# Slot experts: a ring of eight weight buffers that SyncE alone loads, and expert outputs stored by ScalarE

## The chip, the cores and the metric

The kernel runs on one core of one Trainium2 chip. The metric is the device time of one execution, in microseconds (us). PE is TensorE, ACT is ScalarE, DVE is VectorE, POOL is GpSimd and SP is SyncE. Each core has 16 DMA engines. SP, ACT and POOL can each issue a DMA: an instruction that hands the transfer over and returns, with a semaphore raised when the data has landed.

## The reference, cut to what matters

The model is a two-layer audio tower: seven convolutions with layer norms, a state space layer, a routed mixture of 4 experts, a two-way scan, and last a soft mixture of 64 experts. Only the last part is touched. Each expert `n` works on 16 slots of each of 8 batches, so on 128 rows of 192 features:

```python
Xs = jnp.einsum('bmd,bmnp->bnpd', x, D)
hdn = _layernorm(Xs, ln_g[:, None, :], ln_b[:, None, :])
hdn = jnp.einsum('bnpd,ndh->bnph', hdn, w1) + b1[:, None, :]     # 192 -> 384
hdn = jax.nn.gelu(hdn, approximate=False)
Ys = jnp.einsum('bnph,nhd->bnpd', hdn, w2) + b2[:, None, :]      # 384 -> 192
Y = jnp.einsum('bsd,bms->bmd', Ys.reshape(bsz, n * p, d), C)
```

## The kernel before

The program is a sequence of blocks, each with one hand-written instruction stream per engine and a barrier at its end. `dispatch` makes the normalised slot inputs (the tiles `H1`, `H2`), `experts` runs the 64 experts, `combine` mixes their outputs into the result. The change is in `experts`, and makes two of its tiles larger.

An expert's weights come in two transfers, issued by SP in `load` (L1808, L1810): `w12` (480 KB: 128 rows of 3840 bytes, the first 128 rows of w1 and all of w2) and `w1x` (97.5 KB: 65 rows of 1536 bytes, the rest of w1 and the bias row). They go to slot `r` of a ring of `RING = 4`; each slot has a semaphore `expert_loaded{r}`.

Per expert, DVE scales the slot inputs into `a1`, `a2` (L1907). PE does `up(n)`: six matmuls into one of two PSUM banks (L1850, L1851), raising `expert_hid`. ACT does the GELU into `eg` (L1877), raising `expert_act`. PE does `down(n)`: three matmuls (L1858), raising `expert_out`; ACT copies the result from PSUM to slot `r` of `ye` (L1883), raising `expert_read`. The tile goes to `ys` in HBM (L1822, 96 KB). In each stream the order is fixed: PE does `up(n+1)` and then `down(n)`; ACT does the GELU of n+1 and then the copy of n. The copy first waits until the store of expert n-4, from the same slot of `ye`, has landed (`y_stored{r}`). `down(n)` waits for the GELU of n and for the copy of n-2.

SP's loop body for one expert is: wait for `expert_out` of n, load expert n+4 into the slot that is now free, wait for the copy of n, store n. As PE goes to `up(n+4)` after `up(n+3)` and `down(n+2)`, weights are issued some two experts' time before they are wanted.

POOL meanwhile fetches parts of `ectb` (375 KB each, 12 in all) that `combine` will need (L1840). `combine` starts with three loads of `yb` from `ys`, issued by ACT (L1925), and so needs all stores to have landed.

Of the kernel before, what the change touches and what calls it, by code (L numbers as in the profile page):

```python
# [12 lines left out]
P = 128  # L13
B = 8
# [540 lines left out]
D = 192  # L555
D1, D2 = 128, D - 128
# [10 lines left out]
SOFT_E, SLOT, SOFT_H = 64, 16, 384  # L567
SLOTS = SOFT_E * SLOT
SC = SLOTS // P
SHC = SOFT_H // P  # L570
# [1222 lines left out]


RING = 4
MIX_PIECES = 4
MIX_RING = 3


def experts(nc, T, S, io):  # L1800

    ps = T["ps"]
    pH, pY = [ps[0], ps[1]], [ps[2], ps[3]]
    W = SOFT_H + SHC * D
    n_rows = B * SLOT

    def load(sp, n, r):
        sp.dma_start(T["w12"][:, r, :], bass.AP(io["w12"].tensor, n * P * W, [[W, P], [1, W]]))\  # L1808
            .then_inc(S[f"expert_loaded{r}"], 16)
        sp.dma_start(T["w1x"][:, r, :], bass.AP(io["w1x"].tensor, n * (D2 + 1) * SOFT_H, [[SOFT_H, D2 + 1], [1, SOFT_H]]))\  # L1810
            .then_inc(S[f"expert_loaded{r}"], 16)

    with nc.Block() as block:
        @block.sync
        def _(sp):
            for r in range(RING):
                load(sp, r, r)
            def store(sp, n, r):
                sp.wait_ge(S["expert_read"], n + 3)

                dst = bass.AP(io["ys"].tensor, n * SLOT * D, [[SLOTS * D, B], [D, SLOT], [1, D]])
                sp.dma_start(dst, T["ye"][:, r, :]).then_inc(S[f"y_stored{r}"], 16)  # L1822
            with sp.Fori(0, SOFT_E - 2 * RING + 1, RING) as i:
                for r in range(RING):
                    sp.wait_ge(S["expert_out"], i + r + 1)
                    load(sp, i + r + RING, r)
                    store(sp, i + r, r)
            for r in range(RING):
                store(sp, SOFT_E - RING + r, r)
            for r in range(RING):  # L1830
                sp.wait_ge(S[f"y_stored{r}"], 16 * SOFT_E // RING + 16)

        @block.gpsimd
        def _(pool):

            for n in range(MIX_RING * MIX_PIECES):
                pool.wait_ge(S["expert_out"], SOFT_E * (n + 1) // (MIX_RING * MIX_PIECES + 1))
                b, c = n // MIX_PIECES, n % MIX_PIECES * (SC // MIX_PIECES)
                s = slice(c, c + SC // MIX_PIECES)
                pool.dma_start(T["ectb"][:, b, s, :], io["ect"][b][:, s, :]).then_inc(S[f"mix_ahead{b}"], 16)  # L1840

        @block.tensor
        def _(pe):
            def up(n, r, loaded):
                pe.wait_ge(S[f"expert_loaded{r}"], loaded)
                pe.wait_ge(S["slots_ready"], 2 * n + 2)

                for c in range(SHC):
                    o = pH[r % 2][:, c * n_rows:(c + 1) * n_rows]
                    pe.matmul(o, T["w12"][:, r, c * P:(c + 1) * P], T["a1"][:, r, :], start=True, stop=False)  # L1850
                    mm = pe.matmul(o, T["w1x"][:, r, c * P:(c + 1) * P], T["a2"][:, r, :], start=False, stop=True)  # L1851
                mm.then_inc(S["expert_hid"], 1)

            def down(n, r):
                pe.wait_ge(S["expert_act"], n + 1)
                pe.wait_ge(S["expert_read"], n + 1)
                for c in range(SHC):
                    mm = pe.matmul(pY[r % 2][:, 0:D], T["eg"][:, r % 2, c * n_rows:(c + 1) * n_rows],  # L1858
                                   T["w12"][:, r, SOFT_H + c * D:SOFT_H + (c + 1) * D], start=(c == 0), stop=(c == SHC - 1))
                mm.then_inc(S["expert_out"], 1)  # L1860

            def products(i, last=False):
                for r in range(RING):
                    if not (last and r == RING - 1):
                        ahead = (r + 1) // RING
                        up(i + r + 1, (r + 1) % RING, 32 // RING * i + 32 * (1 + ahead))
                    down(i + r, r)
            up(0, 0, 32)
            with pe.Fori(0, SOFT_E - 2 * RING + 1, RING) as i:
                products(i)  # L1870
            products(SOFT_E - RING, last=True)

        @block.scalar
        def _(act):
            def gelu(n, r):
                act.wait_ge(S["expert_hid"], n + RING + 1)
                act.activation(T["eg"][:, r % 2, :], pH[r % 2][:, 0:SHC * n_rows], ACT.Gelu)\  # L1877
                    .then_inc(S["expert_act"], 1)

            def copy(n, r, stored):  # L1880
                act.wait_ge(S["expert_out"], n + 1)
                act.wait_ge(S[f"y_stored{r}"], stored)
                act.activation(T["ye"][:, r, :], pY[r % 2][:, 0:D], ACT.Copy).then_inc(S["expert_read"], 1)  # L1883

            def activations(i, last=False):
                for r in range(RING):
                    if not (last and r == RING - 1):
                        gelu(i + r + 1, (r + 1) % RING)
                    copy(i + r, r, 16 // RING * i + 16)
            gelu(0, 0)  # L1890
            with act.Fori(0, SOFT_E - 2 * RING + 1, RING) as i:
                activations(i)
            activations(SOFT_E - RING, last=True)

        @block.vector
        def _(dve):

            dve.sem_inc(S["expert_hid"], RING)
            dve.sem_inc(S["expert_read"], 2)
            for r in range(RING):  # L1900
                dve.sem_inc(S[f"y_stored{r}"], 16)
            with dve.Fori(0, SOFT_E - RING + 1, RING) as i:
                for r in range(RING):
                    dve.wait_ge(S["expert_hid"], i + r + 1)

                    for name, src, g, rows in (("a1", "H1", "egA", P), ("a2", "H2", "egB", D2)):
                        dve.tensor_scalar(T[name][0:rows, r, :], T[src][:, bass.ds((i + r) * n_rows, n_rows)],  # L1907
                                          T[g][:, 0, bass.ds(i + r, 1)], T[g][:, 1, bass.ds(i + r, 1)], ALU.mult, ALU.add)\
                            .then_inc(S["slots_ready"], 1)


def combine(nc, T, S, io):

    pO = T["ps"][0:2]
    with nc.Block() as block:
# [24 lines left out]
        def _(dve):  # L1940
            def bias(b):
                if b < MIX_RING:
                    dve.wait_ge(S[f"mix_ahead{b}"], 16 * MIX_PIECES)
                dve.wait_ge(S[f"mix_loaded{b % MIX_RING}"], 16 + 32 * (b // MIX_RING))  # L1944
# [30 lines left out]
def program(nc, io):  # L1975
    with ExitStack() as ctx:
# [4 lines left out]
        T, S, made = {}, {}, []  # L1981
# [4 lines left out]
        for name in ("nvar nroot tok_link tok_turned tok_normed tok_back tok_affine tok_projected tok_out "  # L1986
                     "ssm_exp ssm_r ssm_angle ssm_link u_ready u_turned uT_ready ssm_in Bu_ready x_ready "
                     "ssm_out y_ready ssm_nlink ssm_slink ssm_blink rows_loaded weights_loaded small_loaded readout_loaded v_ready "
                     "v_turned vT_ready scores_ready mask_ready "
                     "z_ready ez_ready gate_link xh_ready xh_turned two_out "  # L1990
                     "n_ready proj_read proj_done conv_read conv2_done y2_ready two_done two_nlink two_link "
                     "sig phi_link phi_sum phi_root q_ready lg_read q_turned qT_ready "
                     "lg_done xs_read edt_ready lt_done ht_read ed_read ed_turned ect_read ect_turned xs_done "
                     "hat_ready xs2_padded ht_done lg_max lt_max ect_stored0 ect_stored1 xvar xroot soft_nlink rzd_ready "
                     "xs_link expert_out slots_ready expert_hid expert_act expert_read y_stored0 y_stored1 y_stored2 y_stored3 "
                     "soft_loaded mixed mix_out stored0 stored1 stored2 stored3 yb_ready mix_loaded0 mix_loaded1 mix_loaded2 expert_loaded0 "
                     "expert_loaded1 expert_loaded2 expert_loaded3").split():
            S[name] = ctx.enter_context(nc.semaphore(name))
        early_names = ("wt_loaded w0_loaded gram_ready band_loaded w0_split w60_loaded ident_zero identb_ready "
                       "pool_zero dve w0_centred wt_centred w0c_ready w0c_copied gram_done normed l0_ready "  # L2000
# [167 lines left out]
        with ExitStack() as soft:  # L2168
# [24 lines left out]
                dispatch(nc, T, S, io)  # L2193
            def sx(name, shape, dt=F32):
                sb(name, shape, dt, soft)
            sx("w12", [P, RING, SOFT_H + SHC * D])
            sx("w1x", [D2 + 1, RING, SOFT_H])
            sx("a1", [P, RING, P])
            sx("a2", [D2 + 1, RING, P])
            sx("eg", [P, 2, SOFT_H])  # L2200
# [87 lines left out]
```

## Time and profile before

| what | us |
|---|---|
| median of 3 runs | 2651.62 (2646.96 to 2654.98) |
| the profiled execution, its own time | 2649.04 |
| its span in the trace | 2647.2 |
| `experts`, first load issued to last matmul | 2365.87 to 2563.14 in the span |
| PE waits in it before L1850, for weights by the trace | 33.4 |
| mean granted clock of TensorE in 2366 to 2564 | 0.93 |

All places in time are microseconds from the start of the span. `experts` is 197 us of it, 7.5%. Nothing ahead of it is touched, and of `combine` behind it only the line numbers.

### The profile page before, as it was taken

How to read it: one execution, taken by the hardware profiler on the slowest of the kernel's cores; microseconds unless marked ns; L12 is line 12 of the kernel's file. 1: busy time of each engine (PE TensorE's matmuls, PEld its weight loads, DVE VectorE, ACT ScalarE, POOL GpSimd, SP SyncE). 2: the span in 40 equal slices, each digit the busy share in tenths (PEclk: the TensorE clock that was granted, in tenths of full speed). 3: DMA queues.
4: the chain of work that ended last, by engine and by line, in shares of the span. 5: the costliest groups of instructions: out<-in, count | busy, mean ns of one | idle time of the engine just before them, and what ended most of it. 6: DMA issues, size and time to landing. Idle time of an engine off the chain costs nothing. (4 is left out here: it accounts for less than half of the span.)

```text
span 2647.2 us, 47616 instructions
## 1 busy us (share of the span) xinstructions
PE 2269.7 (86%) x16381; PEld 2039.6 (77%) x16381; DVE 1419.1 (54%) x3575; ACT 1113.7 (42%) x2070; POOL 868.4 (33%) x758
## 2 busy tenths in 40 slices
PE   0999999999999999999977554598787888868878
PEld 0899999999999999999966334486454666658868
DVE  6565666666666656565635784132674565532112
ACT  0556565656656565656543001111333544522210
POOL 3445454545455555545432222300320000000000
PEclk9999999999999999999978775799898899979989
DMA  1000000000000000000000004200000101028766
GB/s 54 5 3 3 4 3 4 3 4 3 4 3 4 3 4 3 4 3 3 4 2 1 0 3 149 67 19 22 15 18 0 47 36 47 36 77 270 249 202 210
DMA packets 66016, 104.89 MB, mean 40 GB/s; under 512 B 9589, under 2 KB 52255, under 8 KB 64861
## 3 DMA queue, kind: packets, MB, share of 16 engines
q1 hardware_dynamic: 51102, 80.77, 9.4%
q10 hardware_dynamic: 9280, 14.00, 1.6%
q0 software_dynamic: 5568, 9.27, 1.2%
q8 instruction: 37, 0.61, 0.1%
q14 instruction: 29, 0.24, 0.0%
HBM read 75.44 MB, written 28.49 MB: 39 GB/s over the span
## 5 line engine op out<-in xcount | busy, mean ns | idle before, releaser
L255 PE MATMUL banks<-t_wt,t_l 128*128 128x128 f32 x8508 | 1044.6, 276 | 4.1 <-ACT t_l L330 2.9
L255 PEld LDWEIGHTS banks<-t_wt,t_l 128*128 128x128 f32 x8508 | 1014.0, 193 | 18.3 <-ACT t_l L330 4.1
L426 POOL TENSOR_TENSOR t_rstd<-t_var,t_minus_half 128x4 f32<-128x4 f32 (+1 forms) x379 | 366.7, 968 | 628.3 <-DVE t_var L355 628.3
L363 DVE TENSOR_TENSOR t_yn<-banks,t_rstd 128x512 f32<-128x512 f32 (+1 forms) x379 | 249.2, 657 | 344.9 <-POOL t_rstd L426 326.1
L312 ACT ACTIVATE t_sq<-banks 128x512 f32<-128x512 f32 (+1 forms) x379 | 215.9, 570 | 481.7 <-PE banks L255 479.4
L432 POOL TENSOR_TENSOR t_zrstd<-t_zvar,t_minus_half 128x8 f32<-128x8 f32 x196 | 320.8, 1638 | 43.1 <-DVE t_zvar L390 43.1
L343 ACT ACTIVATE t_l<-banks,t_cols 128x512 f32<-128x512 f32 x384 | 292.7, 778 | 47.6 <-PE banks L302 41.9
L352 DVE TENSOR_REDUCE t_ss<-t_sq 128x4 f32<-128x512 f32 (+1 forms) x379 | 244.4, 645 | 112.4 <-ACT t_sq L312 112.3
L330 ACT ACTIVATE t_l<-banks,t_cols 128x512 f32<-128x512 f32 (+2 forms) x381 | 285.1, 748 | 10.9 <-PE banks L264 6.2
L264 PE MATMUL banks<-t_ident,t_yn 128*128 128x128 f32 x1426 | 219.7, 274 | 11.5 <-DVE t_yn L363 10.3
L264 PEld LDWEIGHTS banks<-t_ident,t_yn 128*128 128x128 f32 x1426 | 173.6, 141 | 25.3 <-DVE t_yn L363 11.3
L697 POOL TENSOR_TENSOR t_nrstd<-t_nvar,t_minus_half 125x3 f32<-125x3 f32 x40 | 34.4, 861 | 396.9 <-DVE t_nvar L691 396.9
L302 PE MATMUL banks<-t_p60T,t_w 120*128 120x512 bf16 x384 | 140.3, 386 | 1.1 <-ACT t_l L343 1.0
L1850 PE MATMUL banks<-t_a,t_w 128*128 128x128 f32 x384 | 81.1, 294 | 33.4 <-DMA t_w1x<-in_w1x 33.4
L1907 DVE TENSOR_SCALAR t_a<-t_H,t_egA 128x128 f32 x64 | 22.1, 346 | 148.9 <-PE banks L1851 141.2
L1261 ACT ACTIVATE t_G<-banks 128x384 f32<-128x384 f32 x54 | 26.5, 492 | 168.1 <-PE banks L1222 168.1
L1850 PEld LDWEIGHTS banks<-t_a,t_w 128*128 128x128 f32 x384 | 64.2, 203 | 40.6 <-issue 22.5
L1666 ACT ACTIVATE t_EDT<-banks,t_ltm 128x374 f32<-128x374 f32 x64 | 36.8, 575 | 112.4 <-DVE t_ltm L1772 112.1
L1970 PE MATMUL banks<-t_yb,t_ectb 128*125 128x192 f32 (+1 forms) x384 | 65.8, 334 | 15.0 <-DVE t_yb L1945 10.6
L1851 PE MATMUL banks<-t_a,t_w1x 65*128 65x128 f32 x384 | 78.5, 287 | 0.0
L1970 PEld LDWEIGHTS banks<-t_yb,t_ectb 128*125 128x125 f32 (+1 forms) x384 | 64.1, 192 | 16.7 <-DVE t_yb L1945 10.9
L1858 PE MATMUL banks<-t_w,t_eg 128*128 128x192 f32 x384 | 76.8, 338 | 0.0
(314 smaller groups left out, 3377.1 us busy)
## 6 DMA issues: line engine op xcount, KB each, us to landing
t_w<-in_w SPq DMA_DIRECT2D x64, 480.0 KB
ect<-t_ECT SPq DMA_DIRECT2D x16, 750.0 KB, 3.2
t_ectb<-ect ACTq DMA_DIRECT2D x5, 1500.0 KB, 7.8
t_w1x<-in_w1x SPq DMA_DIRECT2D x64, 97.5 KB
ys<-t_ye SPq DMA_DIRECT2D x64, 96.0 KB
t_yb<-ys ACTq DMA_DIRECT2D x8, 768.0 KB, 10.8
t_ectb<-ect POOLq DMA_DIRECT2D x12, 375.0 KB, 6.1
t_xs<-in_x SPq DMA_DIRECT2D x50, 82.5 KB, 1.9
```

What stands on the lines that cost most here:

```text
L255: mm = pe.matmul(psY[bank][:, t * C:(t + 1) * C], src[:, at:at + P], T["wt"][:, 3 * (layer - 1) + k, :], start=(k == 0), stop=(k == 2))
L264: mm = pe.transpose(psT[:, t * P:(t + 1) * P], T["yn"][:, par, t * C:(t + 1) * C], T["ident"][:, :])
L302: pe.matmul(psL[i % 2][:, :], T["w60"][:, slot, :], p60T[:, 4 * q:4 * q + 4, :].rearrange("r a p -> r (a p)"), start=True, stop=True).then ...
L312: act.activation(T["sq"][:, par, 0:n], psY[bank][:, 0:n], ACT.Square).then_inc(S["squared"], 1)
L330: act.activation(dst, psT[:, 0:n].rearrange("c (t p) -> c t p", p=P), ACT.Gelu, bias=T["cols"][:, 8 + layer:9 + layer], scale=T["cols"][:, ...
L343: act.activation(view(T["l0"][:, :], [[2 * BLOCK, 4], [1, P]], block_at(0, 8 * q + slot)), psL[i % 2][:, :].rearrange("c (a p) -> c a p", ...
L352: dve.reduce_sum(T["ss"][:, par, 0:n], T["sq"][:, par, 0:n * C].rearrange("p (t c) -> p t c", c=C), axis=AX.X)\
L363: dve.tensor_tensor(T["yn"][:, par, 0:n * C].rearrange("p (t c) -> p t c", c=C), psY[bank][:, 0:n * C].rearrange("p (t c) -> p t c", c=C), ...
L426: pool.tensor_tensor(T["rstd"][:, par, 0:n], T["var"][:, par, 0:n], T["minus_half"][:, 0:n], ALU.pow)\
L432: pool.tensor_tensor(T["zrstd"][:, s], T["zvar"][:, s], T["minus_half"][:, 0:POS // 4], ALU.pow)\
L1850: pe.matmul(o, T["w12"][:, r, c * P:(c + 1) * P], T["a1"][:, r, :], start=True, stop=False)
L1970: mm = pe.matmul(pO[k % 2][0:n, 0:D], T["ectb"][:, b % MIX_RING, c, t * TOK:t * TOK + n], T["yb"][:, b % MIX_RING, c, :], start=(c == 0), ...
```

## The change

A second constant, `AHEAD = 8`, is the number of slots for weights; `a1`, `a2` and `ye` keep four (`RING`). SP issues eight loads at the start, then for each n waits for `expert_out` of n and loads n+8. It stores nothing. The store goes to ACT's stream, one expert late: between the GELU of n+1 and the copy of n stands the store of n-1. PE's loop body covers eight experts, ACT's four as before. The two weight tiles grow from 5376 x 4 to 5376 x 8 bytes per partition.

```diff
+AHEAD = 8
         @block.sync
         def _(sp):
-            for r in range(RING):
+            for r in range(AHEAD):
                 load(sp, r, r)
-            def store(sp, n, r):
-                sp.wait_ge(S["expert_read"], n + 3)
-
-                dst = bass.AP(io["ys"].tensor, n * SLOT * D, [[SLOTS * D, B], [D, SLOT], [1, D]])
-                sp.dma_start(dst, T["ye"][:, r, :]).then_inc(S[f"y_stored{r}"], 16)
-            with sp.Fori(0, SOFT_E - 2 * RING + 1, RING) as i:
-                for r in range(RING):
+            with sp.Fori(0, SOFT_E - 2 * AHEAD + 1, AHEAD) as i:
+                for r in range(AHEAD):
                     sp.wait_ge(S["expert_out"], i + r + 1)
-                    load(sp, i + r + RING, r)
-                    store(sp, i + r, r)
-            for r in range(RING):
-                store(sp, SOFT_E - RING + r, r)
-            for r in range(RING):
-                sp.wait_ge(S[f"y_stored{r}"], 16 * SOFT_E // RING + 16)
+                    load(sp, i + r + AHEAD, r)
...
-            def activations(i, last=False):
+            def store(n, r):
+                act.wait_ge(S["expert_read"], n + 3)
+                dst = bass.AP(io["ys"].tensor, n * SLOT * D, [[SLOTS * D, B], [D, SLOT], [1, D]])
+                act.dma_start(dst, T["ye"][:, r, :]).then_inc(S[f"y_stored{r}"], 16)
+
+            def activations(i, first=False, last=False):
                 for r in range(RING):
                     if not (last and r == RING - 1):
                         gelu(i + r + 1, (r + 1) % RING)
+                    if not (first and r == 0):
+                        store(i + r - 1, (r - 1) % RING)
                     copy(i + r, r, 16 // RING * i + 16)
             gelu(0, 0)
-            with act.Fori(0, SOFT_E - 2 * RING + 1, RING) as i:
+            activations(0, first=True)
+            with act.Fori(RING, SOFT_E - 2 * RING + 1, RING) as i:
                 activations(i)
             activations(SOFT_E - RING, last=True)
+            store(SOFT_E - 1, RING - 1)
+            for r in range(RING):
+                act.wait_ge(S[f"y_stored{r}"], 16 * SOFT_E // RING + 16)
...
-            sx("w12", [P, RING, SOFT_H + SHC * D])
-            sx("w1x", [D2 + 1, RING, SOFT_H])
+            sx("w12", [P, AHEAD, SOFT_H + SHC * D])
+            sx("w1x", [D2 + 1, AHEAD, SOFT_H])
```

On SP, in the loop of `experts`, these rows cover two experts before (L1808 and L1810 are the load, L1822 is the store; ISA and REGISTER_ALU rows are waits and address arithmetic):

```order
L1808 ISA
L1808 DMA t_w<-in_w 128x960
L1810 ISA
L1810 DMA t_w1x<-in_w1x 65x384
L1822 ISA
L1822 DMA ys<-t_ye 8x16x192
L1808 ISA
L1808 DMA t_w<-in_w 128x960
L1810 ISA
L1810 DMA t_w1x<-in_w1x 65x384
L1822 ISA
L1822 DMA ys<-t_ye 8x16x192
```

And now, at the same place:

```order
L1809 ISA
L1809 DMA t_w<-in_w 128x960
L1811 ISA
L1811 DMA t_w1x<-in_w1x 65x384
L1821 REGISTER_ALU
L1809 ISA
L1809 DMA t_w<-in_w 128x960
L1811 ISA
L1811 DMA t_w1x<-in_w1x 65x384
```

The store has left SP's stream, so that no load stands behind a wait for the copy.

On ACT, in its loop of `experts`, one expert before (L1877 is the GELU, L1883 the copy):

```order
L1876 REGISTER_ALU
L1877 ACTIVATE t_eg<-banks 128x384
L1881 REGISTER_ALU
L1883 ACTIVATE t_ye<-banks 128x192
L1876 REGISTER_ALU
```

And now (L1868 is the GELU, L1879 the store, L1874 the copy):

```order
L1867 REGISTER_ALU
L1868 ACTIVATE t_eg<-banks 128x384
L1877 REGISTER_ALU
L1879 ISA
L1879 DMA ys<-t_ye 8x16x192
L1874 ACTIVATE t_ye<-banks 128x192
```

The store of the expert before stands between a GELU and the copy that follows it.

## Rows read from the trace of the kernel before

**Rows 1.** The page: span, then busy tenths in 40 slices.

```profile
span 2647.2 us, 47616 instructions
...
PEclk9999999999999999999978775799898899979989
DMA  1000000000000000000000004200000101028766
```

**Rows 2.** DMA issues of 2366 to 2564: KB each, then us to landing.

```profile
t_w<-in_w SPq DMA_DIRECT2D x64, 480.0 KB
t_w1x<-in_w1x SPq DMA_DIRECT2D x64, 97.5 KB
ys<-t_ye SPq DMA_DIRECT2D x64, 96.0 KB
t_ectb<-ect POOLq DMA_DIRECT2D x12, 375.0 KB, 6.1
```

**Rows 3.** Waits of 2360 to 2570: total us, times, longest us.

```profile
ACT t_eg L1877 <- PE banks L1851: 107.5, 64, 5.5
...
PE banks L1850 <- DMA t_w1x<-in_w1x: 33.4, 22, 5.6
PEld banks L1850 <- issue: 22.5, 11, 3.5
```

**Rows 4.** Timeline 2405 to 2412: start, us, engine, line, what.

```profile
2408.11 0.64 SPq L1822 DMA_DIRECT2D ys<-t_ye  x1
2408.20 0.49 ACT L1877 ACTIVATE t_eg<-banks 128x384 f32<-128x384 f32 x1 [1.01 <-PE banks L1851]
...
2409.26 0.33 ACT L1883 ACTIVATE t_ye<-banks 128x192 f32<-128x192 f32 x1 [0.57 <-PE banks L1858]
...
2409.35 0.37 SPq L1808 DMA_DIRECT2D t_w<-in_w  x1
...
2409.91 0.34 SPq L1810 DMA_DIRECT2D t_w1x<-in_w1x  x1
...
2410.32 1.14 PE L1858 MATMUL banks<-t_w,t_eg 128*128 128x192 f32 x6
...
2410.52 0.49 ACT L1877 ACTIVATE t_eg<-banks 128x384 f32<-128x384 f32 x1 [0.93 <-PE banks L1851]
```

**Rows 5.** Timeline of PE, 2470 to 2484, around a wait for weights.

```profile
2478.29 0.48 PE L1850 MATMUL banks<-t_a,t_w 128*128 128x128 f32 x2 [3.26 <-DMA t_w1x<-in_w1x]
...
2479.42 0.64 PE L1851 MATMUL banks<-t_a,t_w1x 65*128 65x128 f32 x2
...
2482.58 0.39 PE L1851 MATMUL banks<-t_a,t_w1x 65*128 65x128 f32 x2
```

**Rows 6.** Stretches: us, busy of PE, PEld, DVE, ACT, POOL, then clock, DMA share, GB/s.

```profile
2380.00:2550.00 170.00, 144.98 (x1048) 138.61 (x1046) 33.88 (x114) 47.69 (x116) 6.70 (x12) 0.97 0.81 261
2367.00:2374.00 7.00, 4.34 (x19) 4.26 (x20) 2.61 (x10) 0.65 (x2) 0.00 (x0) 0.50 0.99 318
2380.00:2398.00 18.00, 16.39 (x124) 15.59 (x123) 4.16 (x14) 5.67 (x14) 0.71 (x2) 1.00 0.85 270
...
2441.00:2451.00 10.00, 8.09 (x60) 7.51 (x59) 2.37 (x8) 2.70 (x7) 0.55 (x1) 1.00 0.89 302
...
2531.00:2541.00 10.00, 7.69 (x57) 7.11 (x56) 2.01 (x8) 2.58 (x7) 0.55 (x1) 1.00 0.87 291
```

**Rows 7.** Timelines at the start and the end of `experts`.

```profile
2365.87 0.33 SPq L1808 DMA_DIRECT2D t_w<-in_w  x1
...
2554.20 0.80 PE L1850 MATMUL banks<-t_a,t_w 128*128 128x128 f32 x2 [2.84 <-DMA t_w1x<-in_w1x]
...
2561.02 2.12 PE L1858 MATMUL banks<-t_w,t_eg 128*128 128x192 f32 x12
...
2566.42 2.76 ACTq L1925 DMA_DIRECT2D t_yb<-ys  x3
```

**Rows 8.** ACT's own DMA issues in `combine`: one of the timeline, and the page's group.

```profile
2591.91 1.02 ACTq L1925 DMA_DIRECT2D t_yb<-ys  x1
...
t_yb<-ys ACTq DMA_DIRECT2D x8, 768.0 KB, 10.8
```

More of the change, by code:

```diff
@@ L1849, in up @@
                     o = pH[r % 2][:, c * n_rows:(c + 1) * n_rows]
-                    pe.matmul(o, T["w12"][:, r, c * P:(c + 1) * P], T["a1"][:, r, :], start=True, stop=False)
-                    mm = pe.matmul(o, T["w1x"][:, r, c * P:(c + 1) * P], T["a2"][:, r, :], start=False, stop=True)
+                    pe.matmul(o, T["w12"][:, r, c * P:(c + 1) * P], T["a1"][:, r % RING, :], start=True, stop=False)
+                    mm = pe.matmul(o, T["w1x"][:, r, c * P:(c + 1) * P], T["a2"][:, r % RING, :], start=False, stop=True)
                 mm.then_inc(S["expert_hid"], 1)
@@ L1862, in products @@
             def products(i, last=False):
[L1863 to L1866, printed above, removed]
+                for r in range(AHEAD):
+                    if not (last and r == AHEAD - 1):
+                        ahead = (r + 1) // AHEAD
+                        up(i + r + 1, (r + 1) % AHEAD, 32 // AHEAD * i + 32 * (1 + ahead))
                     down(i + r, r)
             up(0, 0, 32)
-            with pe.Fori(0, SOFT_E - 2 * RING + 1, RING) as i:
+            with pe.Fori(0, SOFT_E - 2 * AHEAD + 1, AHEAD) as i:
                 products(i)
-            products(SOFT_E - RING, last=True)
+            products(SOFT_E - AHEAD, last=True)
         @block.scalar
@@ L1996, in program @@
                      "soft_loaded mixed mix_out stored0 stored1 stored2 stored3 yb_ready mix_loaded0 mix_loaded1 mix_loaded2 expert_loaded0 "
-                     "expert_loaded1 expert_loaded2 expert_loaded3").split():
+                     "expert_loaded1 expert_loaded2 expert_loaded3 expert_loaded4 expert_loaded5 expert_loaded6 expert_loaded7").split():
             S[name] = ctx.enter_context(nc.semaphore(name))
```

## Prediction

> **What bounds the kernel now.** I read the page first: 40 slices of 66 us each [rows 1]. The 16 DMA engines are nearly idle until slice 37, then show 8, 7, 6, 6 tenths. That last tenth is `experts` and `combine`; the change is in the first, 2365.87 to 2563.14, 197.3 us [rows 7]. So whatever happens, it happens inside 7.5% of the span.
>
> The waits of that stretch come next. PE waits 33.4 us for weights by the trace's attribution, 22 times, up to 5.6 us [rows 3]. The 22.5 us called "issue" on the weight-load side are part of the same halts, seen where no releaser was found. ACT's 107.5 us before the GELU are slack: it waits for PE. So PE and the weights set the pace between them, and the question is how much is PE and how much the transfers.
>
> The timeline of an undisturbed stretch gives PE's own pace: from one GELU to the next is 2410.52 - 2408.20 = 2.32 us per expert, with nothing waited for on PE [rows 4]. 64 experts at that are 148 us. The stage takes 197. The difference, 49 us, is the halts and what they trigger: after a halt of 3.26 us a pair of matmuls takes 0.64 us and not 0.39 until about 2482 [rows 5], that is, TensorE is then granted the lower of its two levels (1.2 GHz, not 2.4), as in the first 7 us (clock 0.50) [rows 6].
>
> Last, the transfers. The stage moves 64 x (480 + 97.5 + 96) KB and 12 x 375 KB [rows 2]: 47604 KB, 48.7 MB. Over 2380 to 2550 the mean is 261 GB/s at a share of 0.81 [rows 6]. 48.7 MB at 261 are 186.8 us: from 2365.87 to 2552.7, which is where the last halt ends (2554.20) to within 1.5 us [rows 7]. The stage is therefore bound by transfers at 261 GB/s. But that is not the rate the engines can hold. Between the halts I find stretches of 270, 291 and 302 GB/s (shares 0.85, 0.87, 0.89), and 318 (0.99) while only loads run [rows 6]. The mean is lower because of a loop: weights are late, PE halts, no slot comes free, SP issues no load, the engines run dry, and the next weights are late again. A load is issued about two paces, 4.6 us, before it is wanted; at 302 GB/s its 591 KB alone are 2 us.
>
> **The change, part by part.**
>
> *Eight slots.* Load n+8 is issued at the end of `down(n)`, six paces (14 us) ahead of need and not two. A halt of PE no longer stops the stream: up to six loads are outstanding. I take it that the engines then run at the backlogged rate through the stage. Its bounds are the weakest and the best of these stretches, 270 and 302 GB/s; I take 288, close to the middle, as the deeper queue also lets a DMA engine that lags be caught up over several loads. 48.7 MB take 180.4, 161.2 and 169.1 us. Against 186.8 that is 6.4, 25.6 and, taken, 17.7 us.
>
> *The end.* Behind the last halt come two experts. At 2554.20 the clock is at its lower level (0.80 us for the first pair) and PE ends at 2561.02 + 2.12 = 2563.14, 8.9 us later [rows 7]. With waits of some tenths of a us per expert (2.64 us pace against 2.32) and no halt of several us, I expect the upper level, and two paces and one `down` of 1.0: 5.6 us. Gain 3.3, or 0 if the last wait is long again.
>
> *The stores leave SP.* SP issues 0.37 + 0.34 + 0.64 us per expert [rows 4], 1.4 of 2.32: it is not full, and no load was held by it for more than the store's 0.65. Gain nothing of its own; the bytes are the same. The Trainium skill (DMA: Bandwidth & Descriptors, section on issuing engines not being separate DMA queues) says that DMAs of all issuing engines run on the same 16 DMA engines and interleave, so that spreading them saves issue time alone. No row here shows one stream of stores on two queues; by the rule this part is worth nothing, and the sum has it at nothing.
>
> *The stores enter ACT.* One issue of 0.64 us per expert [rows 4], behind the GELU. ACT then has 0.49 + 0.64 + 0.33 = 1.46 us and gaps of some 0.1, in a pace of 2.32 or more: it fits. The wait for `expert_read` is met, since that copy is one GELU back. What stands behind the store is the copy of n: it begins now at 2409.26; a store from 2408.69 (end of the GELU) to about 2409.4 makes it 0.2 us late. `down(n+2)` wants that copy more than two us later. Price 0. It would cost something above some 1.4 us per issue, when the next GELU is late.
>
> *The copy's wait for its slot.* The store of n-4 is now issued just before the copy of n-3, so it has three paces, 7 to 8 us, to land. Nearest row: an `ectb` piece of 375 KB on POOL's own queue, among loads, lands in 6.1 us [rows 2]; the store is 96 KB, but in rows of 768 bytes. Lower bound some 2 us, upper 10.8 (`yb`, 768 KB in rows of the same 768 bytes, behind 1500 KB) [rows 8]. I take 5, nearer the first: no cost.
>
> *Start and barrier.* The first four loads are issued at the same moments, the next four behind them; PE's first expert is not sooner. At the end ACT stores expert 63 behind its copy, as SP did; 0. POOL's and DVE's streams are the same, and `combine` waits for the same.
>
> Sum: 17.7 + 3.3 = 21.0 us. The profiled execution of 2649.04 becomes 2628.0 (stage end about 2542). It lay 2.6 under the median of 2651.62, so the median would be 2630.6; I write 2630. With the two bounds: 25.6 + 3.3 = 28.9 gives 2623, 6.4 + 0 gives 2645.
>
> **The rivals.**
>
> *A. PE becomes the bound.* If stores and loads on two queues fill each other's pauses, the rate may reach the 318 GB/s of loads alone: 153 us, and PE's 148 plus a cold start (first GELU to full clock, some 7 us more) are then longer. The end of `experts` would be about 2369.7 + 148.5 + 5 = 2523: 40 us gained, 2611. For it: the stretch at 318. Against it: no stretch with stores in it passes 302.
>
> *B. The engines that carry the stores are full already.* The share with stores in the mix never passes 0.89, and is 0.99 without [rows 6]: some engines may be full while others idle, and then a deeper queue changes nothing about the full ones. The stage stays at 261 to 265 GB/s; what is left is the tail and 0 to 2.8 us: 0 to 6 us, 2646 to 2652. Against it: in the same mix 291 and 302 GB/s were reached for 10 us each. The Trainium skill (the same page, section on why a DMA increments its semaphore by 16) says that a transfer uses the largest number of engines up to 16 that divides the slowest dimension of both sides; by that, the store with its 8 batches goes over 8 engines and `w1x` with 65 rows over 13. The trace agrees as far as it goes: full engines beside idle ones would give such shares of 0.85 to 0.89.
>
> *C. Slower: ACT waits for the landing of a store.* ACT stands still at the copy of n until the store of n-4 has landed, the GELU of n+2 is behind it, and `down` behind that. With six loads outstanding the engines are never free for the stores. If landing takes L, the pace cannot be below about (L + 0.8) / 3. It decides against the change where that passes the present 187/64 = 2.92 us, so from L = 8.0. At the 10.8 us of [rows 8] the pace is 3.87 us, 61 us more: 2713. An issue held up has the same effect: one on ACT took 1.02 us [rows 8], still under 1.4. Against it: the `ectb` pieces, on a queue of their own among the same loads, land in 6.1 us with four times the bytes.
>
> **How the numbers follow.** The forecast (270 to 302 GB/s) has 0.62, A and what lies between 0.13, B 0.16, C 0.09. A measurement of this kernel cannot tell 0.3%, 8 us, from no change. The forecast's own range is 2623 to 2645; to leave out no more than 2 in 10, I go down to A's 2611 and up to 2647, into B. Faster by over 0.3% (below 2643.7): nearly all of the forecast, and A: 0.75. Within: most of B and the forecast's edge: 0.16. Slower: C, 0.09.
>
> **What would show it.** In the profile after: GB/s over the middle of the stage near 288 and the share near 0.87 or above (B: unchanged 261, 0.81; A: 300 or more); the wait of PE for weights spread over many short ones, each under 1 us, and the clock at 1.00 in the stage after its first 10 us; ACT's copy released by PE and not by a landing of `ys` (C: a group `t_ye <- DMA ys` in the waits); SP's issues six experts ahead of need; the last matmul of `experts` near 2542. The prediction is wrong if the rate does not rise although loads are always outstanding, or if ACT's waits name a DMA.

## The result

The changed kernel takes 2609.01 us (median of 4 runs, 2607.57 to 2610.53) against 2649.29 us (4 runs, 2644.31 to 2654.98): 40.3 us less, ratio 0.9846, 95% interval 0.9830 to 0.9863. The forecast was 2630, from 2611 to 2647: the direction was right, the gain nearly twice what was forecast, and the time lies 2 us below the range. It is where rival A put it (2611).

The profiled execution took 2607.57 us, its span is 2605.8. The end of the page's slices, which answers to [rows 1], first; then the stretches of the stage (us, busy of PE, PEld, DVE, ACT and POOL, clock, DMA share, GB/s), which answer to [rows 6]:

```profile
span 2605.8 us, 47552 instructions
...
PEclk9999999999999999999988775599899799988999
DMA  1000000000000000000000004200000001016976
```

```profile
2380.00:2510.00 130.00, 130.00 (x1012) 130.00 (x1011) 33.44 (x113) 46.31 (x113) 6.15 (x11) 1.00 0.98 331
2367.00:2374.00 7.00, 4.21 (x18) 3.92 (x19) 2.52 (x10) 0.55 (x2) 0.00 (x0) 0.50 0.99 328
```

The first row is the finding: in 130 us PE is busy for 130 us, at a clock of 1.00. The transfers run at 331 GB/s, where the stretches of before with stores in them [rows 6] stood at 261 to 302. That is not their limit but what PE asks for: (480 + 97.5 + 96 + 70) KB per expert, 761.7 thousand bytes, every 2.31 us are 329 GB/s.

The waits of 2378 to 2524 (total us, times, longest us) answer to [rows 3]:

```profile
ACT t_eg L1868 <- PE banks L1842: 60.6, 62, 2.0
ACT t_ye L1874 <- PE banks L1849: 29.1, 57, 0.7
ACT t_ye L1874 <- DMA ys<-t_ye: 4.7, 6, 1.0
```

PE has no row: it waits for no weights once the first experts are through. A new row says that ACT waited six times for a store to land, 4.7 us in all. The timeline of ACT (start, us, engine, line, what) answers to [rows 4]:

```profile
2400.78 0.49 ACT L1868 ACTIVATE t_eg<-banks 128x384 f32<-128x384 f32 x1 [1.01 <-PE banks L1842]
2401.00 0.62 ACTq L1879 DMA_DIRECT2D ys<-t_ye  x1
2401.76 0.33 ACT L1874 ACTIVATE t_ye<-banks 128x192 f32<-128x192 f32 x1 [0.49 <-PE banks L1849]
2403.10 0.49 ACT L1868 ACTIVATE t_eg<-banks 128x384 f32<-128x384 f32 x1 [1.01 <-PE banks L1842]
2403.31 0.62 ACTq L1879 DMA_DIRECT2D ys<-t_ye  x1
2404.43 0.33 ACT L1874 ACTIVATE t_ye<-banks 128x192 f32<-128x192 f32 x1 [0.85 <-DMA ys<-t_ye]
```

From GELU to GELU it is 2.32 us, PE's pace. The store's issue of 0.62 us begins 0.22 us into the GELU, and ends before the copy's input is there. In the second expert the copy is 0.35 us late because a store had not landed; the next GELU is not.

The end of the stage answers to [rows 7]:

```profile
2520.96 2.12 PE L1849 MATMUL banks<-t_w,t_eg 128*128 128x192 f32 x12
...
2526.51 2.90 ACTq L1927 DMA_DIRECT2D t_yb<-ys  x3
```

First load to last matmul is 2365.77 to 2523.08, 157.3 us in place of 197.3. So 40.0 of the 41.4 us that the span lost come from this stage; what follows it takes 82.7 us instead of 84.1.

### The profile page after: what moved, and what is told of

The parts are those of the page before. It is cut to its first block and busy times, and to the rows that moved or that the text cites. A ratio compares the mean times of both kernels' runs of the same rounds, so it can differ in the third digit from the quotient of the medians.

```text
span 2605.8 us, 47552 instructions
## 1 busy us (share of the span) xinstructions
PE 2256.0 (87%) x16381; PEld 2032.9 (78%) x16381; DVE 1420.5 (55%) x3575; ACT 1112.1 (43%) x2070; POOL 867.4 (33%) x758
## 5 line engine op out<-in xcount | busy, mean ns | idle before, releaser
L1772 DVE TENSOR_REDUCE t_ltm<-banks 128x1 f32<-128x374 f32 x64 | 34.8, 544 | 76.8 <-PE banks L1556 76.8
## 6 DMA issues: line engine op xcount, KB each, us to landing
t_w1x<-in_w1x SPq DMA_DIRECT2D x64, 97.5 KB
```

## The experiments

Theory D (depth): before, a load had two paces from issue to use, which is about what it takes to land; more loads outstanding removed the halts. Theory Q (queue): stores in order between the loads on SP's queue kept the rate down. The rival to both is B of the prediction: the DMA engines that carry stores are full.

### e1_depth: eight slots, stores left on SP

```diff
...
             with sp.Fori(0, SOFT_E - 2 * AHEAD + 1, AHEAD) as i:
                 for r in range(AHEAD):
                     sp.wait_ge(S["expert_out"], i + r + 1)
                     load(sp, i + r + AHEAD, r)
+                    store(sp, i + r, r % RING)
...
```

`store` is SP's function of the kernel before, and ACT's stream is as it was before.

> Eight slots for weights, but the stores stay on SP behind each load, as before. Theory D (depth): what raised the rate is that six loads are outstanding instead of two, so PE never halts; then this is about 2609 us, PE at 2.31 us per expert and 330 GB/s in the stage. Theory Q (queue): what raised it is that stores no longer stand in SP's queue between the loads; then the stage stays between 270 and 302 GB/s as in the stretches of before, PE still waits for weights, and this is 2620 to 2645 us.

Measured 2612.05 us (2609.80 to 2614.06), ratio 0.9862 (0.9828 to 0.9897). Depth alone gives nine tenths of the gain. Its rate is not the 330 GB/s that theory D expected, though. The stretch 2380 to 2500, and the waits of 2376 to 2527:

```profile
2380.00:2500.00 120.00, 116.51 (x891) 115.02 (x890) 29.08 (x98) 35.47 (x96) 5.60 (x10) 1.00 0.97 315
```

```profile
ACT t_ye L1883 <- DMA ys<-t_ye: 84.1, 48, 2.7
...
PEld banks L1858 <- ACT t_eg L1877: 6.5, 9, 0.9
ACT t_eg L1877 <- PE banks L1851: 6.2, 7, 1.0
PE banks L1858 <- ACT t_eg L1877: 4.8, 9, 0.7
```

ACT waits 84.1 us for stores to land, against 4.7 in the changed kernel. ACT's slack ahead of the GELU is gone (6.2 us for 60.6), and PE waits for the GELU. This is rival C's mechanism, at a small price: from GELU to GELU it is 2.47 us on average in 2380 to 2500, against 2.32. The stages end at 2527.3 and 2523.1. They are only 4.2 us apart because e1_depth is 3.4 us ahead at its fourth expert.

How long a store takes can be read from the semaphore events of the traces: from its issue to the last of its increments, median of experts 8 to 59. It is 9.4 us here and 7.2 in the changed kernel. The 84.1 against 4.7 us of waiting overstate that difference. Two later runs have eight slots for weights and their stores on ACT, as the changed kernel has, and in the same window (2376 to 2527) their profiles, e4_lead6 first and e9_mix5 second, show

```profile
ACT t_ye L1878 <- DMA ys<-t_ye: 37.9, 26, 2.9
```

```profile
ACT t_ye L1876 <- DMA ys<-t_ye: 61.6, 42, 2.8
```

with stores that land after 7.7 and 8.4 us. A store issued on ACT has about 7.7 us until the copy that needs its slot (from 2401.00 to a copy three paces behind that of 2401.76). So a landing that is half a us longer turns few waits into many, and PE still waits no more than 1.2 us for a GELU in either of the two.

### e2_queue: four slots, stores on ACT

```diff
-AHEAD = 8
+AHEAD = 4
```

> Stores on ACT as in the changed kernel, but four slots for weights. Theory D: about 2649 us, halts as before. Theory Q: 2625 us or less, with a rate above 290 GB/s. A mixture: between them, and e1_depth then says how much depth gives alone.

Measured 2647.59 us (10 runs), ratio 0.9995 (0.9981 to 1.0010): no difference that these runs can tell. In 2380 to 2500:

```profile
2380.00:2500.00 120.00, 102.85 (x728) 97.89 (x727) 23.94 (x81) 33.32 (x81) 4.51 (x8) 0.96 0.81 260
```

260 GB/s at a share of 0.81, as before [rows 6]. Theory Q falls as the explanation of the 40 us: with two paces of lead, moving the stores changes nothing, and the stores take 5.1 us to land against 4.9 before (semaphore events again).

### e3_lead5 and e4_lead6: the lead alone

Slots and streams of the changed kernel; SP loads n+5, or n+6, at the end of expert n.

```diff
...
-                    load(sp, i + r + AHEAD, r)
+                    load(sp, i + r + LEAD, (r + LEAD) % AHEAD)
...
```

> The changed kernel with SP one load ahead of what four slots allow: load n+5 is issued at the end of expert n, three paces (6.9 us) ahead of need. In the profile of the changed kernel a load landed 4.4 to 4.7 us after its issue. Theory D, in the form that a lead need only cover a load's landing: nearly all of the gain, 2612 to 2620 us. If the whole depth of eight is needed to average lagging DMA engines: 2630 us or more.

> The same with load n+6, four paces (9.3 us) ahead of need. Theory D, lead covers landing: 2609 to 2612 us, no halts. If the full depth is needed: 2620 us or more.

| loads ahead | lead before use | time, us | ratio, interval | GB/s, 2380 to 2500 |
|---|---|---|---|---|
| 4 (e2_queue) | 2 paces | 2647.59 | 0.9995 (0.9981 to 1.0010) | 260 |
| 5 (e3_lead5) | 3 paces | 2612.88 | 0.9868 (0.9835 to 0.9902) | 315 |
| 6 (e4_lead6) | 4 paces | 2607.94 | 0.9846 (0.9812 to 0.9879) | 323 |
| 8 (the change) | 6 paces | 2609.01 | 0.9846 (0.9830 to 0.9863) | 331 |

Issuing one load further ahead takes the rate from 260 to 315 GB/s and brings 35 of 40 us; the second brings the rest; the seventh and eighth bring nothing. In e3_lead5 the waits of 2376 to 2530 that are left for weights are

```profile
PE banks L1845 <- DMA t_w1x<-in_w1x: 3.0, 5, 0.9
PEld banks L1845 <- DMA t_w1x<-in_w1x: 1.1, 1, 1.1
```

five, and one ahead of a weight load of PE, none above 1.1 us, where before there were 21 of up to 3.3 us in 2376 to 2564, and one of 5.6 ahead of the first expert [rows 3]. e2_queue and e3_lead5 differ also in the number of slots and in the experts that one loop body covers; no run has eight slots and two paces of lead. But the trace of e2_queue puts PE's halts down to weights, 21.0 us in 15 waits of 2376 to 2527, and these are what e3_lead5 has lost.

The semaphore events of the traces show why one pace is worth so much. An expert's weights are there when both of its transfers have landed, counted here from the issue of `w12` (experts 8 to 59); loads in flight are issued and not yet landed, on average over 2380 to 2500:

| run | lead, us | weights land, us: median, longest | loads in flight | PE's waits for weights, 2376 to 2527 |
|---|---|---|---|---|
| before | 4.6 | 5.5, 7.8 | 1.9 | 17, and 10 called "issue" |
| e3_lead5 | 6.9 | 6.4, 7.7 | 2.6 | 5 |
| e4_lead6 | 9.3 | 7.0, 8.0 | 2.9 | none |
| the change | 13.9 | 6.8, 8.6 | 2.9 | none |

Before, the median landing alone is longer than two paces; with the halts it is 2.97 us from GELU to GELU (mean of 2380 to 2500), and two of those are 5.9. Three paces cover the median but not the longest, four cover all. That is theory D in the form "the lead must cover the landing". The landing of 4.4 to 4.7 us from which the expectation of e3_lead5 was reasoned is too short: it is 6.8 us there, so the three paces of 6.9 were only just enough, and the nearly full gain of e3_lead5 was less safe than it was made out to be. Nor do eight slots put six loads in flight. There are about three, and the others lie landed in their slots.

### e5_fast_pe and e6_fast_pe_sp: what the transfers can do

Both leave out the matmul with `w1x` in `up`, so the last 64 of 192 features and the bias are not computed. PE's own pace is then 1.64 us per expert (its last ones are that far apart); the bytes are the same. e6_fast_pe_sp has its stores on SP.

```diff
...
-                    pe.matmul(o, T["w12"][:, r, c * P:(c + 1) * P], T["a1"][:, r % RING, :], start=True, stop=False)
-                    mm = pe.matmul(o, T["w1x"][:, r, c * P:(c + 1) * P], T["a2"][:, r % RING, :], start=False, stop=True)
+                    mm = pe.matmul(o, T["w12"][:, r, c * P:(c + 1) * P], T["a1"][:, r % RING, :], start=True, stop=True)
...
```

> The changed kernel without the second matmul of each pair in up (the one with w1x: it leaves out the last 64 of 192 features and the bias). PE's pace would be 1.6 us per expert, ACT's about 1.8; the bytes are the same, 0.76 MB per expert. It measures what the transfers can do when PE does not hold them back. If the step of the prediction that took 288 GB/s was right but for the queue, the rate stays near 330, which is what PE asked for, and the pace at 2.3. If transfers had room, the rate goes above 350 GB/s and the pace below 2.2 us.

> The same reduction, with the stores on SP's queue behind the loads and eight slots. Theory Q in what is left of it: on one queue the transfers cannot reach the same rate, and the pace is 0.1 us per expert or more longer than in e5_fast_pe. Theory D alone: the same rate within 2%.

One execution each: 2605.59 and 2609.79 us, beside 2647.28 of the kernel before. A third of PE's matmuls is gone and the time is the same within 3.5 us. Stretches of the two:

```profile
2380.00:2500.00 120.00, 93.61 (x604) 85.69 (x603) 29.70 (x100) 36.19 (x98) 5.61 (x10) 1.00 0.97 329
```

```profile
2380.00:2500.00 120.00, 94.19 (x585) 84.84 (x584) 29.24 (x99) 35.36 (x96) 5.61 (x10) 0.99 0.95 318
```

329 and 318 GB/s. Neither of the two expected outcomes came (2.3 us at near 330, or below 2.2 above 350). My reading of the changed kernel, that PE alone held it, is incomplete: something else holds nearly the same pace. The waits of e5_fast_pe name it:

```profile
ACT t_ye L1873 <- DMA ys<-t_ye: 88.1, 52, 3.0
PEld banks L1848 <- ACT t_eg L1867: 37.6, 45, 2.0
PE banks L1848 <- ACT t_eg L1867: 28.8, 41, 1.8
```

It is not the weights. ACT waits for stores to land, 88.1 us, and PE for ACT. ACT's 98 activations in 120 us are 49 experts, 2.45 us each, where the changed kernel has 104, 52 experts at 2.31. A store lands 7.2 us after its issue in the changed kernel and 8.9 here (medians), with 2.9 and 3.6 loads in flight on average; what makes it slower is not shown. e5_fast_pe is ahead at the start, where PE is at the lower clock and has fewer matmuls: its sixth GELU starts at 2382.19, that of the changed kernel at 2386.89. It loses this in the middle and gains again over its last experts, where no loads are left: the last GELU starts at 2518.80 against 2521.16.

Between one queue and two (e6 and e5) the rates differ by 3% and the stretch by one expert of 49: less than theory Q's 0.1 us per expert, more than the 2% of D alone. Two single executions do not decide it; e1_depth, with more runs, has the same 4 us.

### e7_wide_fast and e8_wide_ring4: stores whose two sides begin with 128

`ys` is laid out expert by expert, so a store is 128 rows to 128 rows, and `combine` loads each batch in eight pieces. e7_wide_fast is e5_fast_pe with this, e8_wide_ring4 the kernel before with it.

```diff
...
-                dst = bass.AP(io["ys"].tensor, n * SLOT * D, [[SLOTS * D, B], [D, SLOT], [1, D]])
+                dst = bass.AP(io["ys"].tensor, n * P * D, [[D, P], [1, D]])
...
```

> As e5_fast_pe, but ys is laid out with the 128 rows of an expert outermost, so that both sides of a store have 128 as their slowest dimension (combine then loads yb in eight pieces per batch, so only the stage of the experts is compared). Rival B's mechanism: a store of before runs on 8 of the 16 engines, which are the full ones; spread over 16, the pace falls by 5% or more against e5_fast_pe and 512 more small packets are seen. If the engines that carry stores are not what limits, the pace is the same.

> The kernel before (ring of four, stores on SP) with the same layout of ys. If full store engines made the weights late, the stage of 197 us is shorter by 5 us or more; by theory D it is the lead that is short, and the stage stays within 3 us.

e7_wide_fast took 2604.10 us in one execution. Its stretch, its packets of 2366 to 2510, and its waits of 2360 to 2500 are

```profile
2380.00:2500.00 120.00, 105.67 (x691) 93.13 (x689) 33.25 (x112) 47.03 (x115) 6.69 (x12) 1.00 1.03 364
```

```profile
DMA packets 24387, 48.80 MB, mean 339 GB/s; under 512 B 3072, under 2 KB 15424, under 8 KB 24384
```

```profile
PE banks L1841 <- DMA t_w1x<-in_w1x: 20.6, 21, 5.3
...
ACT t_ye L1873 <- DMA ys<-t_ye: 7.9, 7, 2.1
```

364 GB/s against 329. ACT makes 115 activations in the 120 us where e5_fast_pe makes 98, a pace of 2.09 us against 2.45, 15% less. The wait for stores falls from 88.1 to 7.9 us, and now weights are waited for: they land after 12.5 us (median), with 5.8 loads in flight, and six paces of 2.09 are 12.5. The packets of the changed kernel, 2366 to 2530:

```profile
DMA packets 24530, 49.32 MB, mean 301 GB/s; under 512 B 2560, under 2 KB 15565, under 8 KB 24525
```

The 3072 small packets are 512 more than these 2560, eight per store. That fits the Trainium skill (DMA: Bandwidth & Descriptors, section on why a DMA increments its semaphore by 16), by which each engine of a transfer posts its own completion and the slowest dimensions of the two sides set how many engines there are: 8 for the store as it is, 16 for this one. The semaphore events agree: a store's semaphore rises in 9 steps in the changed kernel, which is 8 and one for the rest, and in 16 in e7_wide_fast. But the edit changes more than the number of engines. The expert's rows now lie in one piece of HBM and not in eight, and ACT's issue takes 0.34 us and not 0.62. Which of these is worth how much of the 15% no run separates.

e8_wide_ring4 took 2669.43 us in one execution. Some 13 us of what it lost are behind the experts, in `combine` with its eight pieces; but the stage of experts is no shorter either: it ends at 2568.17 + 2.12 = 2570.3 and not 2563.1.

```profile
2380.00:2500.00 120.00, 103.11 (x700) 98.89 (x700) 23.19 (x78) 32.07 (x78) 4.52 (x8) 0.91 0.76 244
```

With two paces of lead, spreading the stores does not help. I expected within 3 us and saw 7 more, in one execution whose halts fall otherwise; I leave that difference open. What the two together say is that the new layout counts where many loads are in flight; nothing shows that the stores set the pace of the kernel before.

### e9_mix5 and e10_again: the ring's memory given to combine

After the experts the memory of the weights is freed, and `combine` gets five slots in place of three. e10_again is the changed kernel on the same chip.

```diff
...
-                    act.wait_ge(S["mixed"], TPB * (b - MIX_RING + 1))
+                    if b >= MIX_SLOTS:
+                        act.wait_ge(S["mixed"], TPB * (b - MIX_SLOTS + 1))
...
```

> The changed kernel, and after the experts their ring of weights (43 KB per partition) is freed and gives combine two more slots, five in place of three, so that the loads of batches 3 and 4 start with combine and not when slots come free. The chain of the changed kernel shows 12.5 and 12.6 us of yb landings in combine, but PE waits there for only 3.7 us behind its first matmul, and is busy 59 of 66 us. If waiting time of PE counts: 1 to 4 us faster than the changed kernel, 2605 to 2608. If the chain's landings count: 10 us or more, below 2600. Against both: five batches loading at once slow batch 1's landing.

> The changed kernel once more, unedited, beside e9_mix5 on the same chip: 2607 to 2611 us.

Measured 2604.77 us (2602.71 to 2607.06, 5 runs), ratio 0.9831 (0.9815 to 0.9847); e10_again 2608.13 (2606.81 to 2611.36), ratio 0.9845 (0.9829 to 0.9861). The medians are 3.4 us apart, within what PE's waits allowed (1 to 4 us) and far from the 25 us of the chain's landings; the intervals overlap, so the size is uncertain. In the two profiled executions the experts end at 2522.18 and 2522.07, and what follows takes 79.2 and 84.2 us, so the difference lies in `combine`. It is the fastest of the complete kernels by its median.

## Why the prediction was right and where it was wrong

**What bounds.** That the stage, not the rest, would move, that weights were late, and that a load issued two paces ahead is the cause: right. e3_lead5, with one pace more of lead, is 35 us faster than e2_queue. What the prediction never priced is the landing: it set two paces, 4.6 us, against 2 us of bytes, and the weights took 5.5 us at the median to land.

**The rate, 288 GB/s out of 270 to 302.** This is the step that failed. The prediction took the rate between halts [rows 6] for what "the engines can hold". Those stretches came from a kernel that issues its loads two paces ahead and had 1.9 in flight on average; they show what that gives, with or without a halt. With one pace more the whole stage runs at 315, above the best of those stretches; with eight slots at 331, which is demand; with demand raised and the stores laid out anew, at 364. At 331 GB/s the 48.7 MB take 147 us, and PE with its 148 us is as long, so PE's pace and not the transfers ended the gain. The term was set at 17.7 us; with the end's 3.3 taken off the measured 40.0 it was some 36.7. A premise failed with it: "up to six loads" were to be outstanding, and there were 2.9 on average. The row that was closer to the truth stood in the same group: 318 GB/s while four loads were outstanding and no store ran. I read it as "without stores". The stretches at 331 and 364 have their stores in them, so stores do not keep the rate at 302.

The trace of before could have told this. Its stretches of 10 us and more average over dips; two shorter ones, again with stores in them (SP issues one at 2399.00), are

```profile
2398.50:2403.50 5.00, 4.03 (x29) 3.44 (x27) 1.19 (x4) 1.44 (x4) 0.02 (x1) 1.00 0.97 331
2443.50:2450.50 7.00, 5.09 (x38) 4.51 (x37) 1.12 (x5) 1.58 (x5) 0.00 (x0) 1.00 0.92 326
```

So "no stretch with stores in it passes 302", which was held against rival A, was a matter of the stretches chosen.

**The end, 3.3 us.** Right in kind: the end is at the upper clock, 2.32 us per expert to the last. Both terms together were 21.0 and measured 40.0.

**The stores leave SP: nothing.** Right with four slots (0.9995). With eight it is not quite nothing: e1_depth is at 2612.05 and e4_lead6, with stores on ACT, at 2607.94, both measured beside the same runs of the kernel before. Stores that follow the loads in one queue took 9.4 us to land, those on ACT's queue 7.2 to 8.4. The moment of their issue moved too, so the queue's own part is not separated. The rule of the Trainium skill that the prediction drew on (DMA: Bandwidth & Descriptors, section on issuing engines not being separate DMA queues), by which the DMAs of all issuing engines share the same 16 DMA engines, agrees with the rates at four slots, 260 GB/s against 261.

**The stores enter ACT: nothing.** Right, and with more room than thought: the issue overlaps the GELU.

**The copy's wait.** Taken as landing in 5 us against 7 to 8 allowed. It was 7.2 us, so the term was mis-sized, and it is in part luck that it cost nothing: ACT waited six times, 4.7 us in all, and PE never. The margin of some 0.5 us was gone in e4_lead6 and e9_mix5, where ACT waited 37.9 and 61.6 us, and the same wait becomes the limit in e5_fast_pe.

**Rival A** (0.13) came true in its number and in PE as the bound. Its sum, PE's 148 us and a cold start, gave 2611, and its reason, two queues filling each other's pauses, is not shown: e1_depth on one queue gets within 4 us of it. **Rival B** was wrong about the kernel before, and its mechanism fits what e7_wide_fast shows: once PE is faster, the other layout of the stores takes the pace from 2.45 to 2.09 us. In the changed kernel PE's pace hides it. **Rival C**'s mechanism is in e1_depth at 3 to 4 us.

The range ended where A did. A's own sum had the end of the stage right (2523; measured 2523.08). The 2 us by which the time lies below it come from the median of before, from which A took its 40 us: it was 2651.62 over three runs and is 2649.29 over four. A range that ends at a rival's own estimate leaves no room for that rival's scatter.

## What to carry to other kernels

The rate of a ring that runs dry, read over stretches of 10 us and more, was here a product of how far ahead it loads and not what the DMA engines can do: 302 GB/s at best where they later gave 331 and 364. Look for short stretches, and for those in which more is outstanding. Compare the lead, from a load's issue to its use, with the longest landing of all that the use waits for, by its semaphore: here three paces of 2.31 us instead of two were worth 35 us, and more than four nothing. And when an engine reaches 100%, take work off it in an experiment: here a third fewer matmuls brought 3.4 us, and the waits named stores that land late.

## What the runs showed of the hardware that I had not expected

- The DMA share is no measure of what is left. It was 0.93 at 315 GB/s in e3_lead5, 0.97 at 315 in e1_depth, 0.98 at 331 and 1.03 at 364.
- A DMA that ACT issues is taken up while its previous activation still runs: the issue of 0.62 us began 0.22 us into a GELU of 0.49.
- With a third of PE's matmuls left out, stores of 96 KB with 8 as the slowest dimension of one side, beside 577.5 KB of loads, landed in 8.9 us and held the pace at 2.45; with 128 on both sides it was 6.0 and 2.09. ACT's issue of the first kind took 0.62 us, of the second 0.34.
- One issue on SP took 1.24 us, not 0.41, with the loads of five experts issued ahead of it at the start. It delayed nothing, since SP had only loads to issue.
